# Query and probability transposes of a cross-attention kernel: from TensorE to 32x32 blocks on VectorE and an exchange through DRAM

## The reference

```python
x = x + _L0_xattn_ref(_layernorm(x), ctx, Wq, bq, Wk, bk)        # one head over 128 context rows
x = x + _L0_ffn_ref(_layernorm(x), W, b, A, B, gate_w, gate_b)   # dense layer with routed low rank
x = x + _L1_xattn_ref(_layernorm(x), ctx, mask, q_w, k_w, v_w, o_w, q_norm_w, k_norm_w)
x = x + _L1_ffn_ref(_layernorm(x), gate_*, up_*, down_*)         # int4-like weights, 512 -> 1792 -> 512
```

```python
q = (hidden @ q_proj_w.T).reshape(B, Q, 32, 128).transpose(0, 2, 1, 3)   # 32 query heads of 128
k, v = ...                                                               # 8 key and value heads, repeated 4 times
q, k = rmsnorm(q, q_norm_w), rmsnorm(k, k_norm_w)
scores = einsum('bhqd,bhkd->bhqk', q, k) * scale + mask                  # scale = 1 / sqrt(128)
attn = softmax(scores)
out = einsum('bhqk,bhkd->bhqd', attn, v).transpose(0, 2, 1, 3).reshape(B, Q, 4096)
return out @ o_proj_w.T
```

## Time and profile before

| | before |
|---|---|
| median of three runs | 934.72 us |
| lowest, highest | 934.57, 934.75 us |
| profiled execution: span from first to last instruction | 932.8 us |
| mean granted TensorE clock | 0.999 of full speed |
| TensorE matmul busy | 907.9 us, 97% |
| VectorE, ScalarE, GpSimd busy | 561.5, 508.6, 404.3 us (60, 55, 43%) |
| DMA | 59.21 MB, mean 63 GB/s |

### The profile page before, as it was taken

One profiled execution on the slowest core, in us unless ns is written; L12 is line 12 of the kernel. 1 busy time (PEld: TensorE's weight loads), 2 busy tenths in 40 slices (PEclk: granted clock), 3 DMA queues, 4 the chain that ended last, 5 costly groups with the idle time before them and its releaser, 6 DMA issues.

```text
span 932.8 us, 14521 instructions
## 1 busy us (share of the span) xinstructions
PE 907.9 (97%) x4608; PEld 751.1 (81%) x4608; DVE 561.5 (60%) x944; ACT 508.6 (55%) x1776; POOL 404.3 (43%) x428
## 2 busy tenths in 40 slices
PE   6899999999999999999999999999999999999996
PEld 5786887777888888888888888888888778888885
DVE  6416414233655555555555555555567888988987
ACT  4543760245666666666666666666666444444442
POOL 4333441323544444444443444444434256565662
PEclk9999999999999999999999999999999999999999
DMA  7511011110211111111110111111302033344302
GB/s 253 169 35 58 13 34 46 46 38 10 67 35 35 35 35 35 34 27 30 34 34 34 34 34 34 34 34 46 147 1 79 1 124 121 150 157 157 145 14 91
DMA packets 24689, 59.21 MB, mean 63 GB/s; under 512 B 3069, under 2 KB 3325, under 8 KB 24638
## 3 DMA queue, kind: packets, MB, share of 16 engines
q1 hardware_dynamic: 24638, 58.61, 19.0%
HBM read 56.50 MB, written 2.10 MB: 63 GB/s over the span
## 4 chain that ended last, share of the span: by engine, by line
PE 85%; DVE 7%; POOL 2%; issue 2%; ACT 2%; DMA 1%; SPq 0%; DVEq 0%; ACTq 0%; POOLq 0%
PE bank L1079 20%; PE bank L1081 20%; PE bank L1080 20%; PE bank L1318 6%; PE bank L1290 3%; PE bank L1326 3%; PE bank L1247 2%; PE bank L1248 2%; PE bank L1276 2%; PE bank L1277 2%; DVE st L765 1%; PE bank L1096 1%; DMA resid<-in_x_dram 1%; PE bank L1197 1%; PE bank L1134 1%
## 5 line engine op out<-in xcount | busy, mean ns | idle before, releaser
L574 ACT ACTIVATE sq<-bank 128x128 f32<-128x128 f32 x320 | 84.0, 277 | 141.6 <-PE bank L1081 141.6
L398 POOL TENSOR_TENSOR split<-raw,split 128x512 fp32r<-128x512 f32 x89 | 114.8, 1295 | 89.0 <-ACT split L530 88.9
L910 DVE SCALAR_TENSOR_TENSOR score<-bank,mask_sb 128x512 f32<-128x512 f32 x64 | 44.3, 691 | 130.8 <-PE bank L1318 130.7
L1079 PE MATMUL bank<-split,xnT_hi 128*128 128x512 f32 x288 | 120.8, 420 | 0.6 <-POOL split L398 0.6
L480 POOL TENSOR_TENSOR prob<-prob,rinv 128x512 f32<-128x512 f32 x64 | 66.8, 1044 | 117.5 <-DVE rinv L926 117.5
L648 ACT ACTIVATE prob<-score,nmax 128x128 f32<-128x128 f32 x256 | 99.8, 391 | 27.4 <-DVE nmax L914 27.4
L1081 PE MATMUL bank<-split,xnT_lo 128*128 128x512 f32 x288 | 113.2, 393 | 0.0
L1080 PE MATMUL bank<-split,xnT_hi 128*128 128x512 f32 x288 | 112.4, 390 | 0.0
L1079 PE MATMUL bank<-split,aoT_hi 128*128 128x512 f32 x256 | 106.4, 416 | 0.8 <-POOL split L398 0.8
L1081 PE MATMUL bank<-split,aoT_lo 128*128 128x512 f32 x256 | 100.7, 393 | 0.0
L412 POOL TENSOR_TENSOR msq<-ssq,eps 128x4 f32<-128x4 f32 x80 | 15.9, 199 | 195.4 <-ACT sq L574 195.4
(11 more groups left out here) (143 smaller groups left out, 2185.4 us busy)
## 6 DMA issues: line engine op xcount, KB each, us to landing
raw<-in_wqo_dram SPq DMA_DIRECT2D x64, 256.0 KB, 2.6
kv<-in_ffn_w_dram SPq DMA_DIRECT2D x14, 768.0 KB, 4.4
kv<-in_ffn_z_dram SPq DMA_DIRECT2D x14, 768.0 KB, 5.7
kv<-in_up_s_dram SPq DMA_DIRECT2D x14, 256.0 KB, 5.9
resid<-in_x_dram SPq DMA_DIRECT2D x2, 1024.0 KB, 8.6
kv<-in_ctx_dram SPq DMA_DIRECT2D x1, 2048.0 KB, 10.5
raw<-in_wkey_dram SPq DMA_DIRECT2D x8, 256.0 KB, 3.9
raw<-in_wval_dram SPq DMA_DIRECT2D x8, 256.0 KB, 2.6
```

The costliest lines, as they stand in the source:

```text
L398: pool.tensor_tensor(chunk_dst(c, 1), chunk_raw(c), as32(chunk_dst(c, 0)), ALU.subtract).then_inc(s_lo, 1)
L574: done = act.activation(sq[:, tile(h)], src[:, tile(h)], ACT.Square, scale=float(P) ** -0.5, accum_out=ssq[:, par, h:h + 1])
L910: dve.scalar_tensor_tensor(out=heads(score[:]), in0=heads(bank[2][:]), scalar=SCALE1, in1=mask_sb[:].unsqueeze(1).to_broadcast([P, REP, P] ...
L1079: pe.matmul(dst, l_hi, r_hi, start=first, stop=False)
```

## The change

The eight TensorE transposes of a step go, and so do both of their PSUM banks. VectorE turns the 32x32 blocks of the query product and of the probabilities (`dve.transpose`, two instructions of 512 columns a step) into a buffer `tb`. A 128x128 transpose also needs the blocks themselves exchanged between the four groups of 32 partitions. That is done by DMA through a DRAM scratch: four writes of 128 KB (32 partitions each, runs of 1 KB) and one read of 512 KB (128 partitions, rows of 4 KB) a step, carrying the query of step i together with the probabilities of step i-3 (`PLAG`). The result lands in one buffer, `land`.

Around it:

- The query is 6 iterations ahead of the output (`LEAD`) instead of 3, scores and exponential 4 instead of 2.
- The query is no longer normalised before its transpose: its factor is applied to the scores, one `scalar_tensor_tensor` of 128 columns for each head, in place in PSUM; the maximum and exponential read PSUM.
- The high part of the weights moves from ScalarE to VectorE (`weight_hi`), `probT_lo` and `vcur_lo` from VectorE to GpSimd.
- `headT` and `probT_hi` are made by ScalarE from `land` (SBUF) instead of PSUM.
- Query, scores and their sums of squares have two PSUM banks or buffers each.
- Six value products (instead of three) stand between the first iterations, the weights of a group have two chunk buffers instead of four, and the last iterations and the layer norm of the fourth block are laid out anew.

The core of the diff:

```diff
+LEAD = 6
+PLAG = 3
+WARM = 3
@@ sync
+            def bounce_write(c):
+                cols = bounce_columns(c)
+                if c < STEPS:
+                    sp.wait_ge(s_tq, c + 1)
+                if c >= PLAG:
+                    sp.wait_ge(s_tp, c - PLAG + 1)
+                if c >= 2:
+                    sp.wait_ge(s_br, 16 * (c - 1))
+                for quad in range(KT):
+                    rows = slice(32 * quad, 32 * (quad + 1))
+                    sp.dma_start(scr[c % 2][:, :, quad, cols].rearrange("d e c -> e d c"),
+                                 tb[rows, c % 2, :].rearrange("e (d c) -> e d c", d=KT)[:, :, cols]).then_inc(s_bw, 16)
+            def bounce_read(c):
+                cols = bounce_columns(c)
+                sp.wait_ge(s_bw, 16 * KT * (c + 1))
+                if c >= 1:
+                    sp.wait_ge(s_qt, min(c, STEPS))
+                if c >= PLAG + 1:
+                    sp.wait_ge(s_ptl, c - PLAG)
+                sp.dma_start(land[:].rearrange("p (b c) -> p b c", b=KT)[:, :, cols],
+                             scr[c % 2].rearrange("d e b c -> (d e) b c")[:, :, cols]).then_inc(s_br, 16)
+            def step(j):
+                if 0 <= j < STEPS - 11:
+                    group_chunk(11 + j)
...
+                if 0 <= j + LEAD - 1 < STEPS + PLAG:
+                    bounce_read(j + LEAD - 1)
+                if j + LEAD < STEPS + PLAG:
+                    bounce_write(j + LEAD)
...
+            for j in range(-LEAD, STEPS - 2):
+                step(j)
+                if j in (STEPS - 11, STEPS - 10):
...
+                    load_unit(par, par)
@@ gpsimd, in the order of its step
+                    pool.wait_ge(s_pt, at(p, i) + 1)
+                    pool.tensor_tensor(by_head(probT_lo[:]), landed[:, :, 1], as32(by_head(probT_hi[:])),
+                                       ALU.subtract).then_inc(s_ptl, 1)
...
+                    pool.wait_ge(s_ri, at(p, i) + 1)
+                    pool.tensor_tensor(cur, cur, over(rinv[:, 0:REP], P), ALU.mult).then_inc(s_pn, 1)
...
+                    weight_lo(10 + j, p)
...
+                    pool.tensor_tensor(rms[:, i % 4, :], msq[:, i % 2, :], mhalf[:, 0:REP], ALU.pow).then_inc(s_rr, 1)
...
+                    pool.tensor_tensor(vcur_lo[:], val[:, bass.ds(g * P + (i % T) * NKV * P, P)], as32(vcur_hi[:]),
+                                       ALU.subtract).then_inc(s_vl, 1)
@@ vector
+                dve.tensor_copy(chunk_dst(WGRP + n, 0), raw[:, n % 2, :]).then_inc(s_wh, 1)
...
+                    dve.transpose(blocks_of(i % 2, 0), split32(bank[i % 2][:])).then_inc(s_tq, 1)
...
+                    dve.wait_ge(s_pn, at(p, i) + 1)
+                    dve.wait_ge(s_bw, 16 * KT * (at(p, i) + 2))
+                    dve.transpose(blocks_of((i + PLAG) % 2, 1), split32(prob[:])).then_inc(s_tp, 1)
...
+                        done = dve.scalar_tensor_tensor(out=cur, in0=cur, scalar=rms[:, i % 4, h:h + 1],
+                                                        in1=mask_sb[:], op0=ALU.mult, op1=ALU.add)
@@ tensor, step
-                    for h in range(REP):
-                        done = pe.transpose(bank[1][:, tile(h)], norm[:, 0, tile(h)], ident[:])
-                    done.then_inc(s_b, 1)
...
-                    for h in range(REP):
-                        done = pe.transpose(bank[3][:, tile(h)], prob[:, tile(h)], ident[:])
-                    done.then_inc(s_d, 1)
...
+                if valid(j + LEAD):
...
+                        done = three(bank[i % 2][:], xnT_hi[:, k, tile(t)], xnT_lo[:, k, tile(t)],
+                                     wbuf(b, 0)[:, k, :], wbuf(b, 1)[:, k, :], k == 0, k == KT - 1)
```

More of the change, by code:

```diff
@@ L109, in cross_attention_ffn, with raw_slot @@
         ind = sb("ind", [P, T, NR - 1])
+        scr = nc.dram_tensor("block_bounce", (2, KT, 32, KT, 2 * P), F32, kind="Internal").ap()
+        norm = tb[:, 0, :].rearrange("p (a n) -> p a n", a=2)
+        score, sq = land[:, 0:D], land[:, D:2 * D]
+        def raw_slot(i):
+            return raw[:, i, :] if i < 2 else tb[:, 1, (i - 2) * D:(i - 1) * D]
         QUART = KT * TOK
@@ L492, in _ @@
                     step(j, p)
-            for j in range(STEPS - BODY, STEPS):
+            for j in range(STEPS - BODY + WARM, STEPS):
                 step(j, None)
@@ L770, in ln_stats, with ln_aggr @@
                     ln_tile_stats(t)
+                ln_aggr(k, first, end)
+            def ln_aggr(k, first, end):
                 for t in range(first, end):
@@ L944, in _ @@
+                if j in (-3, -2, -1) and p is None:
+                    weight_hi(10 + 2 * j, None)
+                    weight_hi(11 + 2 * j, None)
+            for j in range(-LEAD, WARM):
                 step(j, None)
             with dve.Fori(0, STEPS // BODY - 1) as p:
-                for j in range(BODY):
+                for j in range(WARM, WARM + BODY):
                     step(j, p)
@@ L1036, in unit @@
                         sub_gate(i + 1, p)
-            dve.wait_ge(s_add, T + STEPS - 1)
-            ln_stats(3, 1, end=T - 1, done=1)
-            for t in range(HALF, T - 1):
-                ln_norm(3, t)
+            ln_aggr(3, T - 2, T - 1)
+            ln_norm(3, T - 2)
             add_out(STEPS - 1, None)
@@ L1224, in values @@
                 done.then_inc(s_v, 1)
-            for m in range(2 * T - 3):
+            for m in range(T + 2):
                 values(m)
-                if 3 <= m < 3 + T:
-                    ln_transpose(2, m - 3)
+                if m >= 2:
+                    ln_transpose(2, m - 2)
             pe.wait_ge(s_xlo, 3 * T)
@@ L1315, in step, with attend @@
                     pe.wait_ge(s_qt, n + 1)
[L1316 removed]
+                    if p is not None or i >= 2:
+                        pe.wait_ge(s_ex, n - 1)
                     for h in range(REP):
[L1318 removed]
+                        done = pe.matmul(bank[2 + i % 2][:, tile(h)], headT[:, tile(h)],
                                          keyT[:, bass.ds(g * TOK + t * P, P)], start=True, stop=True)
                     done.then_inc(s_c, 1)
[L1321 to L1327 removed]
+                for m in VALUES_AT.get(j, ()) if p is None else ():
+                    values(m)
+                def attend():
+                    i = j + 1
+                    n = at(p, i)
+                    if i == 0 and p is None:
+                        pe.wait_ge(s_ve1, 2 * T - 1)
+                    pe.wait_ge(s_ptl, n + 1)
+                    pe.wait_ge(s_vl, n + 1)
+                    if p is not None or i >= 1:
+                        pe.wait_ge(s_al, n)
+                    three(bank[6][:], vcur_hi[:], vcur_lo[:], probT_hi[:], probT_lo[:], True, True)\
+                        .then_inc(s_e, 1)
+                draining = p is None and j >= STEPS - 3
+                if valid(j + 1) and not draining:
+                    attend()
+                if p is None and j == STEPS - 1:
+                    for t in range(HALF, HALF + 2):
+                        ln_transpose(3, t)
                 if valid(j):
```

391 lines of the change are left out of this document (212 added, 179 removed).

## The result

The changed kernel takes **961.1 us** (median of 4 runs, 960.3 to 961.6) against 934.7 for the kernel before: a ratio of **1.028**, 95% interval 1.027 to 1.029. The forecast was 940 with a range of 906 to 965: the direction and the range held, and the likeliest value was 21 us too low; the forecast's own range, 930 to 950, didn't hold. The profiled execution spans 958.8 us, 26.0 more than before.

The account below looks back on a forecast made before the run. The prediction took TensorE, busy for 97% of the span, as the bound: -51.2 + 35.6 + 3.4 + 5.0 + 8.6 + 4 = +5.4 us on a span of 932.8, so 940 us as the median; range 906 to 965.

Parts of the forecast that it names:

- TensorE, -51.2 us: Removed transposes take 0.80 us off each TensorE step, leaving 7.20; over 64 steps -51.2 us if TensorE stays the bound.
- The circle: Strictly ordered chain over ScalarE, VectorE and GpSimd within one loop step: 7.86 us, +35.6 us of TensorE waits over 54 steps.
- Rival 1: The cast isn't held by GpSimd, so the loop's circle is shorter and the kernel faster: 922 to 902 us; chance 0.36.
- The turns: VectorE's two 32x32 block transposes in each step, taken at 0.60 us spacing each, with bounds of 0.54 and 0.69.
- Rival 2: The turns are dearer than an ordinary VectorE instruction: 962 us at 0.85 to 0.9 each; chance 0.13.
- The exchange: DMA through DRAM in each step: 8.0 us from turn to `land`, about 3.3 us spare, so hidden.
- rival 3: The exchange is late because its last write lands late: at 5.6 us, step 8.4 and 967 us; chance 0.11.
- Start, end and unit loads: Costs outside the ordinary loop steps, in four parts: +3.4, +5.0, +8.6 and +4 us.
- (a): Start: wait before the first query product of about 4.8 us, of which a comparable 1.4 is waited today: +3.4 us.
- (b): Start: iterations -2 and -1 have 3.7 us of TensorE work each, while first probabilities await exchange and circle: +5.0 us.
- (c): End: steps 58 and 59 wait for the circle (+5.4), last exchange, attend and `aoT` follow one another (+3.2): +8.6 us.
- (d): Two unit loads of 1.8 MB are queued ahead of the exchanges of steps 54 and 55: +4 us.

Follow-up runs that it names:

- e1: The changed kernel with VectorE's cast of a weight chunk moved from behind `aoT_lo` to ahead of it: 923.9 us, ratio 0.988 to the kernel before.
- e11: The changed kernel with cast, two value products and drain side jobs moved, fill subtractions on VectorE and the loop written out: 906.3 us, ratio 0.969.
- e8: The kernel before with one of four transposes left in each of the two groups that the change removes, nothing else changed: 893.5 us, ratio 0.955.
- e7: The changed kernel with the query's turn on VectorE done a second time into the same place: 1,000.3 us, ratio 1.070 to the kernel before.
- e9: The changed kernel with each of an exchange's four writes issued twice, once into a scratch nobody reads: 966.9 us, ratio 1.034.
- e5: The changed kernel with 18 useless matmuls in TensorE's wait ahead of the first query product: 958.3 us, ratio 1.025.
- e6: The changed kernel with GpSimd's weight-chunk subtractions of iterations -3 to -1 done on VectorE: 955.1 us, ratio 1.021.
- e10: The changed kernel with the two unit loads issued in pieces behind four exchanges instead of two: 956.8 us, ratio 1.023.
- e3: The changed kernel with GpSimd's FFN jobs and ScalarE's Silu table load of the last iterations moved into idle time: 958.1 us, ratio 1.025.
- e4: The changed kernel with the 48 iterations of the hardware loop written out on all engines but the FFN's: 956.6 us, ratio 1.023.

## Why the prediction was right, and where it failed

- **TensorE, -51.2 us.** Right, a little low: e1's steps and the 7.12 us of e11 say that 0.88 us a step left, not 0.80, and e8 shows that down to 7.32 nothing else stood in the way in the kernel before, whose step was 8.00.
- **The circle, 7.86 us, +35.6 us.** Right in every term, and by e1 and e7 also in kind: taking the cast out took 0.7 us off the step and gave 37.2 us, adding a turn of 0.7 cost 39.2. The cast that GpSimd holds was the term with the least support, one row of another kind of instruction. In the forecast it decided the sign, but with the fill and drain as they are it doesn't: by the prediction's 7.52 for a cast that isn't held, an estimate is 961.1 - 54 x 0.34 = 943, still slower than before. Rival 1 had 0.36 and was wrong. That e1's 923.9 lies by its 922 is chance: e1 has no cast in the circle and a step of 7.1 to 7.2, not 7.52.
- **The turns**, 0.70 and 0.67 us, against bounds of 0.54 and 0.69. Rival 2 is out; that its 962 is near the measured 961.1 is chance.
- **The exchange**: writes of 128 KB land in 2.3 us, the read of 512 KB in 3.2, against 2.5 and 3.6. Hidden, as predicted; e9 rules rival 3 out.
- **The step that failed is "Start, end and unit loads".** (a) +3.4: the wait was right, and its consequence was missed, 2.8 us of low clock (e5), so it is 6.2. (b) +5.0: it is 19.3 - 6.2 = 13.1. I gave GpSimd's chunk subtractions a place in the circle of the loop, but didn't count them in iterations -3 to -1, where two are done in a step; e6 puts 4.7 to 5.4 us on them. TensorE's waits there (1.00, 1.00, 3.17, 1.10, 1.11 and 2.17) are 9.5 us, and about 2.7 us are again low clock, behind the waits of 3.17 and 2.17. (c) and (d) +12.6: outside the fill and the 54 steps the transposes saved 64 x 0.80 - 54 x 0.80 - 2.0 = 6.0 us and 9.8 us of work had left, yet the time rose by 5.5 - 0.9 = 4.6; so they are 20.4. For the unit loads +4 was enough (e10 won 1.4 us in the steps, 4.3 in the median). The drain's chain is about 16 and not 8.6. Of GpSimd's and ScalarE's side jobs (3.0 by e3) and of the low clock I had counted nothing. TensorE is idle for 15.3 us from the output product of step 54 to that of 63 (before, 0.6), and 23 of its 512-column matmuls there take 0.43 us instead of 0.23, or 4.6 us: behind the waits of 2.11 and 5.26 us and from 746.9 on, but not behind those of 2.10 and 1.61.
- **Not in the sum at all: the turn of the hardware loop.** It was in the trace of the kernel before, as two steps of 8.7 us, 16 steps apart, and I read only an ordinary step. It costs 9.80 + 9.53 - 2 x 7.86 = 3.6 us in the changed kernel (4.5 by e4's median) and 1.5 before.
- The parts: fill +10.9, loop +1.9, drain and unit loads +7.8, together 20.6 of the 21 us.

How the 16 us of the drain divide between low clock, ScalarE's order and the exchange was not tried one by one. e9 limits the exchange: with 2.7 us more of it, the last three steps take 23.2 us instead of 22.5. The rest stays open.

## What to carry to other kernels

When work leaves the engine that sets the pace, follow the others once around their strict order: what stands in that circle costs its full time, and the cheapest remedy is often to move one instruction into an idle stretch of the same engine. Do the same sum again for fill and drain, iteration by iteration, because one-off jobs that the loop doesn't have stand there in the same queues, and a deeper pipeline makes more of such iterations. To each wait of several us on TensorE add what the slower clock behind it can cost: here 2.8 us behind a wait of 4.78, while behind waits of about 2.1 us it came in one case and not in another.
